# Weights of two quantised feed-forward stages prepared by GpSimd in an earlier stage and kept in DRAM

## The reference, cut to what matters

```
# third: weights to 4 bits with one scale per matrix, biases on the product scale
sw1 = max(|W1|) / 7;   W1_q = clip(round(W1 / sw1), -8, 7) * sw1      # W1 is 1024 x 256
sw2 = max(|W2|) / 7;   W2_q = clip(round(W2 / sw2), -8, 7) * sw2      # W2 is 256 x 1024
b1_q = clip(round(b1 / (s1 * sw1)), ...) * s1 * sw1                   # b2 likewise
out = quant(relu(quant(x) @ W1_q.T + b1_q)) @ W2_q.T + b2_q

# fourth: weights to -1, 0, 1 with one scale per output row
scale = clip(mean(|w|, axis=-1), 1e-5)
w_q = clip(round(w / scale), -1, 1)                                   # w1 1024 x 256, w2 256 x 1024
```

## Time and profile before

| | |
|---|---|
| median of three runs | 2368.57 us (2367.97 to 2370.36) |
| the profiled execution's own time | 2351.08 us |
| its span in the profile | 2348.4 us |
| TensorE, mean granted clock | 0.80 of full |
| experts of the first mixture | about 206 to 729 us of the span |
| preparation of the quantised attention | about 1268 to 1379 us |
| causal attention | about 2092 to 2240 us |

### The profile page before, as it was taken

The page is one execution under the profiler, slowest core; times in us unless marked ns, Lnnn a source line. Parts: engine busy times, 40 slices in busy tenths (PEclk is TensorE's granted clock), DMA queues, the critical chain, the costliest instruction groups (busy, mean ns, idle before and its releaser), DMA issues. The chain is left out here.

```text
span 2348.4 us, 48779 instructions
## 1 busy us (share of the span) xinstructions
PE 1907.5 (81%) x17593; PEld 1089.6 (46%) x17617; DVE 1671.2 (71%) x2792; ACT 1339.2 (57%) x1808; POOL 866.7 (37%) x730
## 2 busy tenths in 40 slices
PE   3776999999997886899996768888888887658856
PEld 1343656556564564478873432232332323434533
DVE  4776755555555557843346989999999998557875
ACT  3454633333335675643333459999999998445565
POOL 4750000000001460600034437777777778233301
PEclk9887999999997997999998765555555555778988
DMA  7343112212113105312323016666666667010100
GB/s 207 91 174 122 69 65 67 67 67 67 65 68 125 48 3 223 132 42 65 70 70 117 1 36 113 113 111 112 112 113 112 110 113 113 1 72 2 24 17 27
DMA packets 384866, 195.29 MB, mean 83 GB/s; under 512 B 312301, under 2 KB 355311, under 8 KB 382703
## 3 DMA queue, kind: packets, MB, share of 16 engines
q1 hardware_dynamic: 381617, 184.47, 32.8%
q0 software_dynamic: 3072, 8.39, 1.1%
HBM read 94.99 MB, written 23.09 MB: 50 GB/s over the span
## 5 line engine op out<-in xcount | busy, mean ns | idle before, releaser
L2435 POOL CAST qa_pT<-qa_eT 128x2048 bf16<-128x2048 uint8 x256 | 477.6, 1893 | 143.8 <-PE qa_O L2455 127.8
L2501 ACT ACTIVATE qa_e<-qa_scores,qa_nb 128x2048 uint8<-128x2048 f32 x256 | 510.4, 1994 | 4.4
L2445 PE MATMUL qa_S<-qa_kT,qa_qT 32*128 32x512 f16 x1024 | 373.2, 615 | 117.6 <-DVE qa_scores L2512 116.2
L2512 DVE TENSOR_SCALAR_CACHE_REDUCE qa_scores<-qa_S,qa_sq 128x1024 f32<-128x1024 f32 (+1 forms) x256 | 453.4, 1804 | 4.3 <-PE qa_S L2445 3.4
L2445 PEld LDWEIGHTS qa_S<-qa_kT,qa_qT 32*128 32x128 f16 x1024 | 64.7, 108 | 325.7 <-DVE qa_scores L2512 287.9
L1116 POOL MEMSET rms_nothing<- 128x512 f16 x1 | 0.5, 524 | 580.0 <-POOLq L3500 580.0
L973 PE MATMUL moe_G<-hT,moe_W 128*128 (+1 forms) x792 | 193.7, 381 | 7.1 <-DVE moe_zero L941 7.1
L982 PE MATMUL moe_O<-moe_W,moe_ap 128*128 (+1 forms) x1584 | 194.5, 273 | 4.1 <-DVE moe_ap L937 4.1
L913 ACT ACTIVATE moe_ap<-moe_a 128x512 f16<-128x512 f32 x132 | 83.1, 629 | 194.8 <-DVE moe_a L935 194.8
L973 PE MATMUL moe_U<-hT,moe_W 128*128 (+1 forms) x792 | 192.7, 380 | 0.0
L982 PEld LDWEIGHTS moe_O<-moe_W,moe_ap 128*128 128x128 f16 x1584 | 154.4, 98 | 50.6 <-DVE moe_ap L937 3.9
(11 more groups left out here) (438 smaller groups left out, 3377.3 us busy)
## 6 DMA issues: line engine op xcount, KB each, us to landing
moe_wb<-weights_T SPq DMA_DIRECT2D x264, 128.0 KB, 2.8
moe_W<-in_moe_w SPq DMA_DIRECT2D x40, 384.0 KB, 11.8
moe_W<-in_moe_w SPq DMA_DIRECT2D x11, 1152.0 KB, 15.7
moe_xs_rows<-rms_nothing SPq DMA_DIRECT2D x46, 128.0 KB, 1.9
moe_ys_rows<-moe_ys SPq DMA_DIRECT2D x23, 256.0 KB, 2.1
conv_rows<-conv_parts SPq DMA_DIRECT2D x16, 256.0 KB, 3.2
qa_eT<-qa_e SPq DMA_TRANSPOSE x256, 3.1
conv_qst<-conv_rows SPq DMA_DIRECT2D x96, 32.0 KB
```

The costliest lines, as they stand in the source:

```text
L2435: nc.gpsimd.tensor_copy(pT[:, u % RING, :, :].rearrange("p (b r) q -> p b r q", r=2), pairs).then_inc(s_cast, 1)
L2445: last = nc.tensor.matmul(S[:, banks[i], :], qT[rows, g, t * P:(t + 1) * P], kT[rows, g, parts[i] * QW:(parts[i] + 1) * QW], start=True, s ...
L2501: nc.scalar.activation(e8[:, u % RING, :], scores[:, u % RING, :], ACT.Exp, bias=nb[:, p % 2, i:i + 1], accum_out=sums[:, u:u + 1]).then_i ...
L2512: nc.vector.tensor_scalar(target, S[:, banks[0]:banks[-1] + 1, :], sq[:, t, h:h + 1], so_far, ALU.mult, ALU.max, accum_out=greatest).then_ ...
```

## The change

`StagedWeights` is new. Within the experts of the first mixture GpSimd gets a list (`quantise`) that loads the four weight matrices and the biases through its own DMA queue, computes the ternary scales by sums of magnitudes that it halves step by step, quantises everything, and stores the results in DRAM. Each of its operations is followed by a wait for itself (`done`). VectorE contributes the maxima and the reciprocals, between the first and the second chunk of the experts. Before the quantised feed-forward block and the causal attention SP loads the finished weights (`load`), with a wait of SP's at the end of the preparation (`landed`). VectorE's and GpSimd's work on these weights in the two later stages is removed, and so are its f32 buffers there.

```diff
 def experts(nc, sh, m, load, weights_T, gate, name, staged):
+        staged.buffers(ctx)
...
+            @block.gpsimd
+            def _(pool):
+                staged.quantise(pool)
...
                 first_steps(dve, split, step)
                 output(0)
+                staged.maxima(dve)
+                staged.inverses(dve)
                 with dve.Fori(0, NC - 1) as c1:
...
+class StagedWeights:
+    def maxima(self, dve):
+        dve.wait_ge(self.s_ready, 1)
+        for i, weight in enumerate((self.f, self.g)):
+            self.nc.vector.tensor_reduce(out=self.am[:, i:i + 1], in_=weight, axis=AXX, op=ALU.max, apply_absolute_value=True).then_inc(self.s_am, 1)
+        self.nc.vector.reciprocal(self.inverse, self.scale).then_inc(self.s_inverse, 1)
+
+    def inverses(self, dve):
+        dve.wait_ge(self.s_sw, 1)
+        self.nc.vector.reciprocal(self.rsw, self.sw).then_inc(self.s_rsw, 1)
+
+    def quantise(self, pool):
...
+        def sum_of_magnitudes(out, rows):
+            width = KT * F // rows
+            done(nc.gpsimd.tensor_scalar(g, f, 0.0, 2.0, ALU.max, ALU.mult))
+            done(nc.gpsimd.tensor_tensor(g, g, f, ALU.subtract))
+            halves = g.rearrange("p (r w) -> p r w", r=rows)
+            while width > 2:
+                width //= 2
+                done(nc.gpsimd.tensor_tensor(halves[:, :, 0:width], halves[:, :, 0:width], halves[:, :, width:2 * width], ALU.add))
+            done(nc.gpsimd.tensor_tensor(out, halves[:, :, 0], halves[:, :, 1], ALU.add))
+
+        def rounded(tile, least, greatest, out):
+            done(nc.gpsimd.tensor_scalar(tile, tile, MAGIC, greatest, ALU.subtract, ALU.min))
+            if out is not None:
+                done(nc.gpsimd.tensor_scalar(out, tile, least, None, ALU.max))
...
+        load(f1, a["tf_w1"])
+        wait_landed()
+        sum_of_magnitudes(s1, NF)
+        done(nc.gpsimd.tensor_scalar(s1, s1, 1.0 / D, 1e-5, ALU.mult, ALU.max))
+        load(f2, a["tf_w2"])
+        wait_landed()
+        sum_of_magnitudes(s2, KT)
+        done(nc.gpsimd.tensor_scalar(s2, s2, 1.0 / F, 1e-5, ALU.mult, ALU.max))
+        store(self.scales, s2)
+        load(f, a["qf_w1"])
+        load(g, a["qf_w2"])
+        wait_landed()
+        pool.sem_inc(self.s_ready, 1)
+
+        pool.wait_ge(self.s_am, 2)
+        done(nc.gpsimd.partition_all_reduce(self.amx, self.am, P, bass.bass_isa.ReduceOp.max))
+        nc.gpsimd.tensor_scalar(sw, self.amx, 1.0 / 7.0, None, ALU.mult).then_inc(self.s_sw, 1)
+        pool.wait_ge(self.s_inverse, 1)
+        pool.wait_ge(self.s_rsw, 1)
+        for i, (weight, home) in enumerate(((f, self.q1), (g, self.q2))):
+            done(nc.gpsimd.tensor_scalar(weight, weight, rsw[:, i:i + 1], MAGIC, ALU.mult, ALU.add))
+            wait_stored()
+            rounded(weight, -8.0, 7.0, q)
+            store(home, q)
...
+        load(f1, a["tf_w1"])
+        wait_landed()
+        for r in range(NF):
+            done(nc.gpsimd.tensor_scalar(f1[:, r, :], f1[:, r, :], r1[:, r:r + 1], MAGIC, ALU.mult, ALU.add))
+        rounded(f, -1.0, 1.0, None)
+        for part, scale in enumerate((self.h1, self.l1)):
+            for r in range(NF):
+                done(nc.gpsimd.tensor_scalar(n1[:, part, r, :], f1[:, r, :], -1.0, scale[:, r:r + 1], ALU.max, ALU.mult))
+        store(self.n1, g.bitcast(F16))
+        load(f2, a["tf_w2"])
+        wait_landed()
+        for m in range(KT):
+            done(nc.gpsimd.tensor_scalar(f2[:, m, :], f2[:, m, :], r2[:, m:m + 1], MAGIC, ALU.mult, ALU.add))
+        wait_stored()
+        rounded(f, -1.0, 1.0, q)
+        store(self.n2, q)
+        wait_stored()
...
 class QuantisedWeights:
     def load(self, sp):
+        sp.dma_start(self.w1[:, :], self.staged.q1).then_inc(self.s_load, 16)
+        sp.dma_start(self.w2[:, :], self.staged.q2).then_inc(self.s_load, 16)
+        sp.dma_start(self.constants[:, :], self.staged.constants_home).then_inc(self.s_load, 16)
...
 def quantised_attention(nc, sh, a, gate, next_weights):
                     next_weights.load(sp)
+                    next_weights.landed(sp)
...
-                    next_weights.greatest(pool)
                     pool.wait_ge(s_norm, NB)
...
                     low(0)
-                    next_weights.magnitudes(dve, 0)
                     low(1)
-                    next_weights.magnitudes(dve, 1)
                     low(2)
...
                     low(3)
-                    next_weights.scales(dve, next_gate)
                     low(4)
-                    next_weights.divided(dve, 0)
-                    next_weights.rounded(dve, 0)
                     low(5)
-                    next_weights.integers(dve, 0)
-                    next_weights.hidden_bias(dve)
                     low(6)
-                    next_weights.output_bias(dve)
                     low(7)
...
                         queries(p)
-                        if p == 3:
-                            next_weights.divided(dve, 1)
-                        if p == 4:
-                            next_weights.rounded(dve, 1)
-                        if p == 5:
-                            next_weights.integers(dve, 1)
...
 class TernaryWeights:
     def load(self, sp):
-        sp.dma_start(self.f1[:, :, :], self.a["tf_w1"]).then_inc(self.s_f1, 16)
-        sp.dma_start(self.f2[:, :, :], self.a["tf_w2"]).then_inc(self.s_f2, 16)
+        sp.dma_start(self.n1[:, :, :, :], self.staged.n1.rearrange("p (a f d) -> p a f d", a=2, d=D)).then_inc(self.s_n1, 16)
+        sp.dma_start(self.n2[:, :, :], self.staged.n2.rearrange("p (m n) -> p m n", m=KT)).then_inc(self.s_n2, 16)
...
 def causal_attention(nc, sh, a, gate, next_weights):
                     evacuate(t)
-                    if t == 1:
-                        next_weights.first_scales(dve)
...
-                    if t == 12:
-                        next_weights.second_integers(dve)
```

More of the change, by code:

```diff
@@ L837, in _, with experts @@
                     nc.vector.tensor_copy(dst, shifted[:, :, :].unsqueeze(3).to_broadcast([P, NB, NE, rep])).then_inc(s_comb, 1)
-def experts(nc, sh, m, load, weights_T, gate, name):
+def experts(nc, sh, m, load, weights_T, gate, name, staged):
     CT = 512
@@ L1897, in __init__ @@
         self.w2 = sb("w2", [P, self.NF * D], F16)
[L1898 to L1914, removed]
@@ L1983, in quantised_attention, with landed @@
+    def landed(self, sp):
+        sp.wait_ge(self.s_load, 64)
+def quantised_attention(nc, sh, a, gate, next_weights):
     NH, HD = 16, 16
@@ L2019, in quantised_attention @@
             rsv = sb("rsv", [P, KT], F32, inner)
-            next_weights.prepare(inner)
             vT = cf
@@ L2870, in first_halves @@
-    def first_halves(self, dve):
-        nc, chained = self.nc, self.chained
-        self.first_divided(dve, range(0, self.NF // 2))
-        chained(nc.vector.tensor_copy(self.h16[:, :], self.s1[:, :]))
-        chained(nc.vector.tensor_copy(self.h1[:, :], self.h16[:, :]))
-        chained(nc.vector.tensor_tensor(self.l1[:, :], self.s1[:, :], self.h1[:, :], ALU.subtract))
-    def first_divided(self, dve, rows):
-        for f in rows:
-            last = self.nc.vector.tensor_scalar(self.f1[:, f, :], self.f1[:, f, :], self.r1[:, f:f + 1], MAGIC, ALU.mult, ALU.add)
-        self.chained(last)
@@ L2898, in second_divided @@
-    def second_divided(self, dve):
-        nc, chained = self.nc, self.chained
-        for m in range(KT):
-            last = nc.vector.tensor_scalar(self.f2[:, m, :], self.f2[:, m, :], self.r2[:, m:m + 1], MAGIC, ALU.mult, ALU.add)
-        chained(last)
-    def second_rounded(self, dve):
-        self.chained(self.nc.vector.tensor_scalar(self.f2[:, :, :], self.f2[:, :, :], MAGIC, 1.0, ALU.subtract, ALU.min))
-    def second_integers(self, dve):
-        self.nc.vector.tensor_scalar(self.n2[:, :, :], self.f2[:, :, :], -1.0, None, ALU.max).then_inc(self.s_n2, 1)
@@ L3518, in mixture @@
                     route(nc, sh, m, hT, load, a[f"moe{layer}_router"], weights_T[0:m.rows, :], f"moe{layer}_route")
-                experts(nc, sh, m, load, weights_T, sh.gates[:, 2 * layer + 1:2 * layer + 2], f"moe{layer}")
+                experts(nc, sh, m, load, weights_T, sh.gates[:, 2 * layer + 1:2 * layer + 2], f"moe{layer}", staged)
         with own_semaphores(nc):
@@ L3532, in program @@
         with own_semaphores(nc):
-            ternary = TernaryWeights(nc, ctx, a)
+            ternary = TernaryWeights(nc, ctx, staged)
             causal_attention(nc, sh, a, sh.gates[:, 6:7], ternary)
```

203 lines of the change are left out of this document (90 added, 113 removed).

## The result

The changed kernel takes 2417.9 us (median of four runs, 2413.7 to 2423.0), the kernel before 2369.3 us beside it: ratio 1.0203, 95% interval 1.0182 to 1.0224, 48.6 us slower. I had forecast 21 us slower (2390). The profiled execution took 2420.2 us with a span of 2417.5.

What follows compares the result with a forecast made beforehand. TensorE was taken to set the experts' pace. Losses of 17, 2.5, 12.7 and 1 (33 us) less gains of 8 and 2.9 (11) gave plus 22: 2373 profiled, 2390 us with 17.5 carried to the median; range 2365 to 2418.

Steps and rivals of the forecast that it cites:

- the price of the tensor-scalars: GpSimd in the experts: a full 128x2048 f32 tensor-scalar was taken to last 2.0 us.
- GpSimd is dearer: Rival, experts: tensor-scalars cost like tensor-tensors, 4 us more in the sums, 22 in the second chunk; 2417 us, chance 10%.
- First chunk, sums: Experts' first chunk: GpSimd's two sums of magnitudes hold VectorE and make TensorE wait, 17 us lost, ends 0 and 25.
- it waited for them whole: Earlier trace at 1277.17 us: a VectorE shift of 2.39 us was read as waiting out all four GpSimd subtractions.
- the steps of 10.5, 4.8 and 5.4 us: Experts' steps of 3.9 us with VectorE held: first chunk's full operations 10.5, small halvings 4.8, second chunk 5.4.
- Transfers: Experts: 1 MB loads and the stores delay the routing weights, which have 4.3 us in hand; 1 us lost, ends 0 and 8.
- Boundary: End of the first chunk: VectorE's block of reductions and waits delays the next chunk, 12.7 us lost, 4.2 to 14.
- the reload: Chunk's end: GpSimd configures itself again behind the reduction over partitions, 7.0 us before the product for which VectorE waits.
- Second chunk: Experts' second chunk: GpSimd operations hold VectorE beyond each step's slack, 2.5 us lost, ends 0 and 24.
- Preparation: Preparation of the quantised attention: removed VectorE weight work gains 8 us, low end 4.4, high end 19.4.
- The 4.4 us up to the values' turn: Preparation: TensorE's start at 1346.03 us moves to about 1341.6, with ScalarE and TensorE late next; 4.4 us gained.
- Causal attention: Causal attention: eleven iterations without the extra VectorE weight work fall from 7.65 to 7.39 us each, 2.9 us gained, ends 0 and 5.

Runs made afterwards that it cites:

- cheap clips: Changed kernel with GpSimd's 128x2048 minimum or maximum tensor-scalars replaced by multiply-and-add of the same shape and types: ratio 1.0128 to the kernel before.
- no sums: Changed kernel without its two sums of magnitudes, ternary scales set to a constant: experts lose 44.9 us against the kernel before, one execution, no ratio.
- scale on VectorE: Changed kernel with the product with 1/7 made by VectorE behind the reduction over partitions, instead of by GpSimd: ratio 1.0179 to the kernel before.

## Why the prediction was wrong in size

**The step that failed** is the price of the tensor-scalars: "between the cast's 1.9 and the tensor-tensor's 4.1 I take 2.0, since it has one input like the cast". The multiply-and-add is like that (1.97 us). Those with a minimum or a maximum last 5.9 to 7.4 us, beyond my upper bound too. The cheap clips show what it was worth: 20.8 us of the 27.3 by which the experts' loss was too small; most of the other 6.5 are the transfers. The rival "GpSimd is dearer" (2417) has the right cause, but that its time is within a microsecond is luck: it gives the second chunk 24.5 us (17.3 measured) and the sums 21 (17.0), and takes over the transfers' 1 (6.9 alone), the boundary's 12.7 (17.9) and gains of 11 (13.6). 10% was too little for it: with a bound at twice the value taken and no row for the operation itself, it deserved about the chance of the forecast.

- **First chunk, sums: forecast 17, measured 17.0** (no sums). The mechanism is there: at 225.38 us the low half takes 3.50 us beside a GpSimd operation, TensorE waits 2.50. But "it waited for them whole" reads too much into the earlier trace rows: the shift was held for 2.2 us, about one of the four subtractions (2.11 us each), not all of them. That the size fits is partly luck. Where the tensor-scalars are about as short as I had assumed (cheap clips), the sums cost some 14 us (22.5 less 8.3), so the sum was too high there. It had errors both ways: I left VectorE's third operation of each step, L935 with 0.69 us, out of the steps of 10.5, 4.8 and 5.4 us, and the full tensor-tensors take 4.52 and 5.30 us and not 4.1.
- **Transfers: 1 forecast, 6.9 measured**, within the 0 to 8 given. I had taken the 4.3 us in hand as enough, since a 1 MB load lands in about 9 us and a routing weight in 2.8. Loads of 256 KB, one at a time, made it true (0.9 us).
- **Boundary: 12.7 forecast, 17.9 measured.** The block is as forecast (12.6 us), the reload too, and the experiment with the scale on VectorE shows it was on the path. I left out that GpSimd starts at once on whole matrices, and holds the new chunk's first product and first low half: 4.3 us.
- **Second chunk: 2.5 forecast, 17.3 measured.** The failed step, here at full weight. The 2.5 doesn't even follow from its own terms: three steps of 1.5 us, less 1.4 in each of two groups, are 1.7.
- **Preparation: 8 forecast, 10.8 measured.** The 4.4 us up to the values' turn were 6.3 (from the lag of the products), the 3.7 between the queries 3.9; 0.6 lie ahead of the removed work. What is late next is ScalarE, as forecast:

```profile
1418.32 2.29 DVE L2442 TENSOR_SCALAR qa_ints<-qa_cf 128x4096 f16<-128x4096 f32 x1
1421.81 1.01 PE L2280 MATMUL qa_TR<-identh,qa_ints 128*128 128x128 f16 x8 [1.78 <-ACT qa_kT L2344]
```

  The keys' turn in front of it moved by 4.0 us and not by 1.9. Its shorter waits gave 2.1 of them, near the forecast. The other part is that I had read this chain in a stretch at the lower clock. From the last turn of the rows to the keys' turn the first profile of the kernel before takes 6.3 us at a mean granted clock of 0.73, the second one 4.8 us at 1.00, and so do all ten changed kernels. In order, the two windows and three rows of the second profile:

```profile
1326.70:1332.98 6.28, 6.28 (x36) 3.43 (x37) 6.04 (x11) 0.60 (x1) 4.58 (x7) 0.73 0.00 1
1329.61:1334.40 4.79, 4.79 (x36) 2.94 (x37) 4.58 (x9) 0.60 (x1) 3.11 (x5) 1.00 0.02 5
1334.40 1.06 PE L2166 MATMUL qa_TR<-identh,qa_stack 128*128 128x128 f16 x16
1335.03 0.69 DVE L2303 TENSOR_TENSOR hT<-qa_hT_TP,hT 128x512 f16<-128x512 f32 x1
1348.93 1.03 PE L2182 MATMUL qa_TR<-identh,qa_ints 128*128 128x128 f16 x8 [5.28 <-DVE qa_ints L2344]
```

  The keys' turn doesn't wait for the eighth low half, which begins behind it. At the full clock TensorE waits 5.28 us for VectorE's integers instead of 3.95, so more of VectorE's 14.5 us can be gained than I had read.
- **Causal attention: 2.9 forecast, 2.8 measured**; the iterations take 7.4 us, as said.

Direction, places and untouched third and fourth chunks came out as written. The sum of the measured parts is 60.5 less 10.8 and 2.8, 46.9 us, for 48.6 between the medians; the remaining 1.7 us are less than single executions differ by.

## What to carry to other kernels

An idle engine's work is free only if each of its operations, and each of its transfers, is shorter than the slack of the step it shares something with: cut both to that size before judging the move. Price an operation by a row with the same operations in it, not only the same shape and inputs, and where no row has it, give the case of the far bound a full share of the chances. Put what others wait for on the engine that has it first, and start it several steps before it is needed.

## What the runs showed of the hardware that was not expected

- GpSimd's tensor-scalar over 128x2048 f32 takes 1.97 us as multiply-and-add with a scale from memory, 2.21 us with two constants, 5.9 with a maximum alone to f16, 7.1 to 7.5 us with a minimum or maximum beside another operation; plain subtraction to f16 took 5.4 to 5.7 us. The Trainium skill, page "GPSIMD Engine Reference", section 4.1, calls operations with one input "roughly line-rate"; the traces agree for the multiply-and-add (1.97 us) and the cast (1.89 us), beside the 2.28 us of a VectorE reduction of that shape. For the others they do not agree.
- VectorE is let in before the long operation's end. The held subtraction of 441.25 us, less its own 0.69 us, could start at 445.62, 4.4 us after GpSimd's operation began and 2.7 before its shown end; at 404.98 and 482.64 it is 4.4 as well, beside the f16 ones of 5.9 us (394.83, 412.15, 489.81) 4.0. The Trainium skill, page "SBUF — State Buffer", section "Who interferes with whom", has the second to issue blocked until the first finishes. Here the measurement decides: the hold is 4.4 us as beside the tensor-tensor of 4.52 us at 231.00, which is one reason why the rival priced at 4.1 came near although the operations last 7. What ends the hold wasn't tried.
- After the reduction over partitions GpSimd's next ordinary operation came 6.7 to 7.7 us later in the seven profiles in which it followed (6.7 to 7.1 in six, 7.7 in that of no sums), also where VectorE didn't wait for it.
